# Half of an output product inside the chain over states, and Q's second part cut in two

## What is computed

```python
q = silu(x @ Wq.T); k = silu(x @ Wk.T); v = x @ Wv.T       # 16 heads of 32
beta = 2.0 * sigmoid(x @ Wbeta.T)
k = k * rsqrt(sum(k * k) + EPS)                            # per head
def step(S, inp):                                          # over the tokens
    qt, kt, vt, bt = inp
    delta = bt * (vt - einsum('bhk,bhkv->bhv', kt, S))
    S = S + einsum('bhk,bhv->bhkv', kt, delta)
    return S, einsum('bhk,bhkv->bhv', qt, S)
og = o * sigmoid(x @ Wg1.T @ Wg2.T)
og = og * rsqrt(mean(og * og) + EPS) * g_norm              # per head
return og @ Wo.T
```

## Time and profile before

| | |
|---|---|
| median of three runs | 5054.02 us |
| the profiled execution | 5102.55 us, its span 5100.8 us |
| mean granted clock of TensorE in the span | 0.963 of full speed |
| TensorE busy (matmul) | 90% of the span |
| VectorE (DVE) busy | 71% |
| ScalarE (ACT) busy | 47% |
| delta rule layer | about the first 2100 us of the span |

### The profile page before, as it was taken

One profiled execution on the slowest core, in us unless ns is written; L12 is line 12 of the kernel. 1 busy time (PEld: TensorE's weight loads), 2 busy tenths in 40 slices (PEclk: granted clock), 3 DMA queues, 4 the chain that ended last, 5 costly groups with the idle time before them and its releaser, 6 DMA issues.

```text
span 5100.8 us, 144724 instructions
## 1 busy us (share of the span) xinstructions
PE 4587.9 (90%) x63104; PEld 3208.2 (63%) x63104; DVE 3619.3 (71%) x7890; ACT 2408.7 (47%) x4592; POOL 716.7 (14%) x909
## 2 busy tenths in 40 slices
PE   5799999999999998499999999999999999999988
PEld 4677777777777776456546646645654654665564
DVE  3666776666667666276787788778778778867876
ACT  3233433333333333164564565466456457546645
POOL 0000000000000000112211211221221221122121
PEclk9899999999999998699999999999999999999999
DMA  2222222222222222100000000000000000000000
GB/s 61 48 62 67 68 71 64 61 61 61 61 62 61 61 66 68 65 1 18 1 18 17 10 9 18 18 1 18 17 1 18 17 10 10 18 18 1 18 9 9
DMA packets 352134, 171.76 MB, mean 34 GB/s; under 512 B 300016, under 2 KB 300784, under 8 KB 350736
## 3 DMA queue, kind: packets, MB, share of 16 engines
q1 hardware_dynamic: 342528, 145.20, 10.7%
q10 hardware_dynamic: 8976, 17.30, 1.2%
HBM read 93.74 MB, written 67.63 MB: 32 GB/s over the span
## 4 chain that ended last, share of the span: by engine, by line
PE 43%; DVE 10%; ACT 3%; issue 1%; POOL 1%; DMA 1%; SPq 0%; DVEq 0%; ACTq 0%; POOLq 0%
PE row_psum L1698 9%; PE row_psum L1673 9%; PE row_psum L40 5%; DVE smax L1951 5%; PE row_psum L42 5%; PE row_psum L41 5%; PE row_psum L1686 4%; PE row_psum L1742 2%; ACT xr_hi L1325 1%; PE row_psum L1726 1%; PE row_psum L1463 1%; DVE probs L1931 1%; DVE stats L1785 1%; POOL rstd L1268 1%; PE row_psum L1645 1%
## 5 line engine op out<-in xcount | busy, mean ns | idle before, releaser
L1951 DVE TENSOR_REDUCE smax<-row_psum 128x1 f32<-128x512 f32 x2048 | 1269.3, 681 | 90.7 <-PE row_psum L1673 89.2
L1398 ACT ACTIVATE probs<-row_psum 128x512 f32<-128x512 f32 x2048 | 1092.6, 601 | 364.8 <-PE row_psum L1686 345.2
L1673 PE MATMUL row_psum<-k_stack,q_stack 64*128 64x512 f32 (+1 forms) x2048 | 738.0, 437 | 50.6 <-DVE smax L1951 24.5
L1686 PE MATMUL row_psum<-q_stack,k_stack 64*128 64x512 f32 (+1 forms) x2048 | 730.8, 457 | 20.8 <-ACT probs L1398 8.2
L1673 PEld LDWEIGHTS row_psum<-k_stack,q_stack 64*128 64x128 f32 (+1 forms) x2048 | 350.5, 186 | 504.0 <-DVE smax L1951 374.0
L1698 PE MATMUL row_psum<-probs,v_aug 128*32 128x512 f32 x4096 | 539.6, 604 | 1.7 <-ACT av_sb L1414 0.4
L1686 PEld LDWEIGHTS row_psum<-q_stack,k_stack 64*128 64x128 f32 (+1 forms) x2048 | 318.3, 184 | 220.2 <-ACT probs L1398 152.5
L868 DVE TENSOR_TENSOR lane_t<-lane_t,lane_p 128x30 f32<-128x30 f32 (+14 forms) x960 | 318.3, 332 | 33.0
L865 DVE TENSOR_TENSOR lane_p<-lane_t 128x30 f32<-128x30 f32 (+14 forms) x960 | 315.6, 329 | 23.5
L40 PE MATMUL span_bank<-x_hi,w_hi 128*128 128x256 f32 x1024 | 301.6, 295 | 33.6 <-DVE x_lo L841 33.0
L40 PE MATMUL row_psum<-wf_hi,xr_hi 128*128 128x320 f32 (+1 forms) x1024 | 331.1, 323 | 0.5 <-DVE xr_lo L1819 0.3
(11 more groups left out here) (209 smaller groups left out, 9883.8 us busy)
## 6 DMA issues: line engine op xcount, KB each, us to landing
x_sp<-in_x ACTq DMA_DIRECT2D x33, 512.0 KB, 4.1
tri_dram<-tri SPq DMA_DIRECT2D x256, 64.0 KB, 2.0
lane_t<-tri_dram SPq DMA_DIRECT2D x32, 512.0 KB, 4.7
inv_dram<-lane_t SPq DMA_DIRECT2D x32, 512.0 KB, 2.6
inv_b<-inv_dram SPq DMA_DIRECT2D x256, 64.0 KB, 2.3
x_res<-in_x SPq DMA_DIRECT2D x32, 512.0 KB, 3.9
x<-x_res SPq DMA_DIRECT2D x32, 512.0 KB, 3.8
xs<-x SPq DMA_DIRECT2D x16, 1024.0 KB, 5.5
```

The lines of the kernel that those rows point to most:

```text
L1398: act.activation(probs[:, h % PROBS, tt, :], ps[:, m % STACK_BANKS, :], ACT.Exp, scale=float(DH) ** -0.5).then_inc(exp_ready, 1)
L1673: pe.matmul(ps[:, bank, :], q_stack[rows, qt, P * st:P * st + P], k_stack[rows, kv, :], start=True, stop=True).then_inc(max_mm, 1)
L1686: pe.matmul(ps[:, m % STACK_BANKS, :], k_stack[rows, kv, P * tt:P * tt + P], q_stack[rows, qt, :], start=True, stop=True).then_inc(score_m ...
L1951: dve.tensor_reduce(smax[:, g, st:st + 1], ps[:, bank_of("max", NT * g + st), :], AX.X, ALU.max).then_inc(max_ready, 1)
```

## The change

`project_q` takes a list of parts, so that a call can make one half of Q's second part. On TensorE the first half stays where it was, the second half (12 matmuls) goes between `without_state` and `state_inputs`. The second half of the output product goes from there into the chain, between its first and second chunk, and everything between the chunks moves one place on: `key_sums` to between the second and third, and both `project_gate` to between the third and fourth. On DVE `add_residual(behind, 1)` goes from ahead of the three columns "inputs" to behind the first `advance` and its column. No instruction is added or removed on any engine.

```diff
-            def project_q(b, s, n):
-                if n:
+            def project_q(b, s, n, parts=(0, 1)):
+                if n and parts[0] == 0:
                     pe.wait_ge(ksilu_ready, at(b, s, 2, 1))
-                for g in range(2):
+                for g in parts:
                     last = features((BA, BC)[n][:, SPAN * g:SPAN * g + SPAN], 1, 2 * n + g)
-                last.then_inc(qproj, 1)
+                if parts[-1] == 1:
+                    last.then_inc(qproj, 1)
...
                 transitions(*now)
                 if further:
-                    project_q(*further, 1)
+                    project_q(*further, 1, (0,))
                 without_state(*now)
+                if further:
+                    project_q(*further, 1, (1,))
+                state_inputs(*now)
+                chain(*now, 0)
                 if behind:
                     output(*behind, 1, further, ahead)
-                state_inputs(*now)
-                chain(*now, 0)
+                chain(*now, 1)
                 if further:
                     key_sums(*further, 0, behind)
-                chain(*now, 1)
+                chain(*now, 2)
                 if further:
                     project_gate(*further, 0)
-                chain(*now, 2)
-                if further:
                     project_gate(*further, 1, behind)
                 chain(*now, 3)
...
                 invert_ahead("transitions")
-                if behind:
-                    add_residual(*behind, 1)
                 invert_ahead("inputs")
                 advance(*now, 0)
                 invert_ahead("chain0")
+                if behind:
+                    add_residual(*behind, 1)
                 advance(*now, 1)
```

## The result

The changed kernel takes **5097.82 us** (median of 4 runs, 5094.26 to 5108.04), the kernel before 5054.61 us beside it (5053.01 to 5063.09): a ratio of 1.0074, with an interval of 1.0048 to 1.0099. It is slower, by 37 us by the ratio and 43 by the medians.

The account below looks back on a forecast made before the run. TensorE, busy for 90% of the span, was taken to bound the kernel, its waits mostly instruction supply. Supply +29 and the last two steps +2 gave +31 us: 5133.6 profiled, 48.5 lower unprofiled, so 5085 us; range 5034 to 5112.

Parts of the forecast that it names:

- The supply: From L640 through the chain, TensorE waits for instruction blocks: 3.1 us a step against 2.1, so +29 us in 29 steps.
- the stretch: L640 to L701 of each first-layer step: forecast at 22.4 us or more in the mean, against 21.41 before.
- Rival 1: In the chain, instruction fetches are hidden or the supply catches up, so its waits and clock losses go: 4987 us, chance 0.09.
- The price of 3.7 us for a block: At each block's edge, TensorE waits 3.7 us less its own time for the last 253 instructions.
- 20 us or more each: Sign expected at L664 and L674: idle time of class issue grows to this size at both lines.
- a wait of 2.2, or 1.1 in the mean: For a block starting in L674's first half, every second step: only 1.5 us of small matmuls fill it.
- The floor of 10.12 us: Shortest time from L674 to L701, taken as undisturbed; with the earlier stretch's floor, 74 us was the most to gain.
- rival 2: The dense product in the chain keeps the clock up while supply waits stay equal in sum: 5034 us, chance 0.11.
- The clock: From L640 to L701, fewer falls in the chain against a slower output half: 0, ends -0.7 and +0.8 a step.
- one step in four: Output half at 1.2 GHz, 3.0 us more; this often would eat up the 0.7 us a step the clock costs.
- DVE: State adds and the moved residual add in the chain: costed at 0; with that cover gone, 0.4 us a step, +12.
- The last two steps: No Q or gates part L664 and L674, and the output half is lost: up to 1.5 us each, +2 in all.

Follow-up runs that it names:

- the later pair: Both kernels unchanged, profiled again in two lots: the kernel before ran at 5085.31 us (profiled 5081.47), the changed kernel at 5115.88 us (profiled 5102.21).
- the cut of Q alone: Against the kernel before, only the second half of Q's second part moves to behind the products without state; output half unmoved: 5109.32 us, ratio 1.0042.
- the move alone: Against the kernel before, the output half moves into the chain with fillers and DVE's residual add as in the change; Q's second part stays whole: 5143.41 us.
- the kernel with the state wait: The changed kernel with DVE's old order, the second residual add ahead of the inversion columns and the first state add: 5270.54 us, ratio 1.0377.
- the first pair: The first profiled executions of both kernels, unchanged: 5102.55 us for the kernel before, 5096.45 us for the changed kernel.
- The finer spread: Against the kernel before, six of Q's 24 matmuls and three of the output half's 12 go behind chunk 0, DVE as in the change: 5081.71 us, ratio 0.9992.
- The padding: Small matmuls computing nothing, added ahead of K's projection to the order with Q's first part moved: 5062.41 us, ratio 0.9959 against the kernel before.
- the order with Q's first part moved: Against the kernel before, half of Q's first part goes behind the transitions, half of its second part behind chunk 0: 5058.00 us, later 5057.92.

## Why the prediction was right, and where it was not

**The supply (+1.0 us a step, +29).** Right in kind and nearly in size. The waits of class issue at the four lines went from 50.7 to 78.2 us in the later pair, +27.5, and the idle time of the stretch by 24.0. They stand where they were forecast: L665 and L675 in nearly every step, chunk 0's two lines in some. That it is the supply of instructions is shown by their places, which come once in 256 instructions, and by two orders with the same instructions: the cut of Q alone puts 18.0 us at L665, the move alone 60.4 at L675. That 128 instructions fewer give the changed kernel 68 us and the other 27 fits, but moves the edges as well. Rival 1, that the fetches are hidden, falls by these: nothing but small matmuls stands at L665 and L675, semaphores account for two stays at L665, 1.5 us together, and none at L675, and up to 60 us of waits came and went with the dense work beside them. The Trainium skill ("Runtime: NRT & Kernel Launch", Instruction fetch mechanics) calls the cost of a block's edge mostly hidden; for this kernel the trace disagrees, with up to 2.5 us at one edge.

The price of 3.7 us for a block was nearly right: 3.5 us is the median from edge to edge where TensorE stays, its stay included. The waits made from it were too long at L665 and L675, since TensorE itself was at work longer from edge to edge than the 2.8 us of my sum (3.55 less 0.5 to 0.7): 21.4 / 31 = 0.69 us (in the later profile 26.1 / 31 = 0.84) at L675 and 13.1 / 26 = 0.50 (17.2 / 29 = 0.59) at L665, where I had 0.9 for each. The expectation of "20 us or more each" held for one of the two. The edge in chunk 0 made up for it: 33.0 us in 17 stays of after, about 2 us each, in every second step. That was the term "a wait of 2.2, or 1.1 in the mean".

**The floor of 10.12 us was misread.** I took the shortest window of the earlier trace rows for one "where nothing disturbs it". The tail of 6.83 us above, with L675 (1.21) and one chunk (0.87) by the earlier trace rows, makes 8.91: even the shortest window had 1.2 us more than that, 0.94 of them idle (10.12 less 9.18). 350.57 less 28 times 8.91 is 101 us, not 67, and of these 46 are idle (350.57 less 304.11) and 52 are the clock's and not 20, by the busy time weighted with the share not granted. The step that failed is "the other 20 us are left for the clock". With 52 us at stake rival 2 deserved a price of 5002 and more room than I gave it.

**The clock (0, ends -0.7 and +0.8).** It was -0.4 a step in the later pair (12 us in 28 steps), inside my ends, but as the difference of two large terms. The clock never falls any more in chunks 1 to 3: 34 us, 1.2 a step, are won there. The output half pays: 104.23 us in the later profile against 28 times 3.01, 0.7 a step. Against the first profile of before, the longer one, the clock gives back 29 us (52 become 24). I had put "one step in four" at 3.0 us; it is one in two at 1.5. The Trainium skill ("TensorE: Matmul & The Clock Gate", Part 1) has activity release the throttle; the rows agree that the dense product restores it for the chunks behind, and show that the product itself pays for the sparse wait ahead of it. That a wait costs clock in what follows it is shown once more by the kernel with the state wait, behind the output half, where 3.0 us of idle brought 2.05 more of busy time in the chunks.

**DVE (0; with the cover gone +12).** Right for the change as it is: one stay of 0.2 us for the state in the one profile of after, none in the other. The cover is worth more than I said. Had `add_residual` not been moved along, the cost would be some 150 us, as it would then stand ahead of the first state add and wait there for a product that comes behind chunk 0. My 12 us priced DVE being a little late in the new order, which no run showed.

**ScalarE, SP, POOL (0).** The rows for the transitions' copy at L665 (1.5 us) and for `og_both` at L702 (2.3 or 2.4) are nearly the same in both kernels. The attention layers kept their time, as far as their rows were read: 50.5 us of idle ahead of the key products in both of the later pair.

**The last two steps (+2).** 20.75 and 20.70 us in after against 18.37 and 18.97 in before, +4.1; in the later pair +5.3. In kind right, in size half.

**The stretch.** 22.4 us or more in the mean was forecast from 21.41, and was not reached. It was 594.06 / 28 = 21.22, against a profile of before that was itself 48.5 us long; in the later pair 21.59 against 20.86, +0.73 a step. With the last two steps that is some 27 us. What stands ahead of the first window gives 5.2 back, which I had not counted. In the very first step there is no output half, so in the kernel before L664 and L674 stand packed one behind the other, with a stay of 2.20 us ahead of L674 (2.52 in the first pair). The change puts half of Q between them, and the stay is 0.39 us (under 0.2 in the first pair), with one of 0.96 at L665; the first stretch takes 22.49 us in place of 24.10. The rest of the 5.2 I have not placed. The profiled times of the pair differ by 20.7 us, of the 30 to 43 that the unprofiled runs show. The remainder is not placed: the profiled execution of after, again, was the fastest of its six runs (5102.21, median 5115.88), so the median's further 14 us stand in no trace.

**How near was it?** +31 us was forecast and 37 to 43 came. In the 28 windows of the later pair the sum is 24 us of idle, 9 of busy time at full clock and 12 won by the clock; the last two steps add 5 and the first ones take as much. So the supply is right as a cause, and that the total is so near owes something to terms that cancel.

**What I got wrong behind the prediction** were above all two sums for kernels of my own. The finer spread (17 us expected, none) counted what chunk 0 had behind it, where only what stands ahead of an edge feeds it. The padding (25 to 45 us expected, none) took idle time for free room.

## What to carry to other kernels

Idle time of class "issue" inside a run of equal small matmuls is the instruction supply: divide the instructions of a stretch by the packets on the instruction queue, and look at how long TensorE takes for one packet's worth. A dense product of few instructions is what lets the supply catch up, and it must stand ahead of the packed groups; moving one from between two packed groups to behind them frees the later ones and starves the earlier. Before trusting a floor, build it from the distances of a step without any wait, and profile both kernels on one occasion, which the pair used here was not.

## What the runs showed of the hardware

- TensorE's stays of class issue stand at places that come once in 256 of its instructions: all 682 of 0.4 us or more in the first layer, in fourteen profiles. Most such places cost nothing; 46 to 77 of some 350 had a stay in the kernel before again and the changed one again. Where TensorE stays, it is 3.5 us in the median since the last edge.
- A step has 2951 TensorE instructions, 11.5 times 256, and in the changed kernel the lengths of the stretch alternate, 19.41 and 23.00 us in neighbours: every second step has a block's edge in chunk 0 with a stay of about 2 us. In the order with Q's first part moved and 3071, 12 times 256, the alternation is gone (19.15 to 21.39 us in 29 steps), although the profile's page has 514 packets on the instruction queue in place of 499.
- Stays at an edge are up to 2.0 to 2.7 us, and one of them ahead of the output half costs that product mostly 1.0 to 1.5 us by the clock (4.0 to 4.5 in place of 3.0, at a mean clock of 0.62 to 0.73).
- The kernel before gave medians of 5054 to 5086 us on five occasions; differences of 0.5% are told only beside runs of the same lot.
